# Wider spectrum products on VectorE and joined small steps in a 2-layer FFT-attention and FFN kernel

## The reference, cut to what matters

```python
qf = fft(q, axis=2); kf = fft(k, axis=2)
corr = ifft(qf * conj(kf), axis=2).real
w, idx = top_k(corr.transpose(0, 1, 3, 2), topk)
w = softmax(w, axis=-1)
for i in range(topk):
    g = minimum(idx[:, :, None, :, i] + pos, L - 1)
    out = out + w[:, :, None, :, i] * take_along_axis(v, g, axis=2)
x = x + out
```

## Time and profile before

| what | value |
|---|---|
| median of 3 runs (lowest to highest) | 2646.56 us (2642.76 to 2648.35) |
| span of the profiled execution, first to last instruction | 2644.4 us |
| PE busy | 2497.7 us, 94% |
| POOL busy | 2155.5 us, 82% |
| DVE busy | 1901.7 us, 72% |
| ACT busy | 1055.7 us, 40% |
| DMA traffic | 613.19 MB, 232 GB/s mean |

### The profile page before, as it was taken

The page is one execution under the profiler, slowest core; times in us unless marked ns, Lnnn a source line. Parts: engine busy times, 40 slices in busy tenths (PEclk is TensorE's granted clock), DMA queues, the critical chain, the costliest instruction groups (busy, mean ns, idle before and its releaser), DMA issues.

```text
span 2644.4 us, 36606 instructions
## 1 busy us (share of the span) xinstructions
PE 2497.7 (94%) x12288; PEld 1559.9 (59%) x12288; DVE 1901.7 (72%) x4966; ACT 1055.7 (40%) x1906; POOL 2155.5 (82%) x1558
## 2 busy tenths in 40 slices
PE   4999866799999999999999999999999999999998
PEld 3655555566666656666666666666666666654444
DVE  5989989778787788777877788778876688645000
ACT  4788855533443343533443334533333233201000
POOL 5799999778998799988998899888998899654222
PEclk8999978899999999999999999999999999999999
DMA  9399998966788687966887687957786687758853
GB/s 325 99 261 269 269 244 198 231 192 209 254 266 228 219 252 238 277 203 210 258 270 210 217 275 248 271 181 236 253 250 172 219 265 243 199 203 301 268 180 114
DMA packets 550028, 613.19 MB, mean 232 GB/s; under 512 B 322640, under 2 KB 448720, under 8 KB 532176
## 3 DMA queue, kind: packets, MB, share of 16 engines
q1 hardware_dynamic: 549840, 610.86, 76.6%
HBM read 383.22 MB, written 151.00 MB: 202 GB/s over the span
## 4 chain that ended last, share of the span: by engine, by line
PE 53%; POOL 22%; DVE 8%; DMA 7%; SPq 5%; issue 4%; ACT 1%; POOLq 0%; DVEq 0%; ACTq 0%
PE f_ps L840 11%; PE f_ps L844 11%; PE f_ps L842 11%; PE a_ps L718 7%; PE a_ps L805 5%; PE a_ps L763 4%; POOL a_zu L1115 4%; POOL f_x1p L1115 4%; POOL a_rows L1115 3%; DMA a_w_lag<-a_w_row 2%; PE a_ps L821 2%; PE a_ps L820 2%; POOL a_zv L1115 2%; POOL a_zf L1115 2%; PE a_ps L768 1%
## 5 line engine op out<-in xcount | busy, mean ns | idle before, releaser
L840 PE MATMUL f_ps<-f_whi,f_hhi 128*128 128x512 f16 x2048 | 777.3, 380 | 5.6 <-issue 2.4
L844 PE MATMUL f_ps<-f_whi,f_hlo 128*128 128x512 f16 x2048 | 777.4, 380 | 0.0
L842 PE MATMUL f_ps<-f_wlo,f_hhi 128*128 128x512 f16 x2048 | 777.4, 380 | 0.0
L924 ACT ACTIVATE a_side<-a_ps 128x256 f32<-128x256 f32 (+1 forms) x320 | 128.0, 416 | 873.5 <-PE a_ps L805 698.4
L844 PEld LDWEIGHTS f_ps<-f_whi,f_hlo 128*128 128x128 f16 x2048 | 200.6, 98 | 242.3 <-issue 1.1
L842 PEld LDWEIGHTS f_ps<-f_wlo,f_hhi 128*128 128x128 f16 x2048 | 200.7, 98 | 230.8 <-issue 1.1
L840 PEld LDWEIGHTS f_ps<-f_whi,f_hhi 128*128 128x128 f16 x2048 | 200.7, 98 | 220.6 <-issue 6.7
L1115 POOL TENSOR_TENSOR a_prod<-a_prod,a_tf 128x512 f32<-128x512 f32 x128 | 160.2, 1273 | 138.7 <-DVE a_tf L1242 138.7
L1115 POOL TENSOR_TENSOR a_zv<-a_zv,a_tw 128x512 f32<-128x512 f32 x128 | 183.3, 1450 | 100.5 <-DVE a_tf L1242 100.5
L805 PE MATMUL a_ps<-inv,a_prod 128*128 128x256 f32 x1024 | 239.5, 388 | 25.6 <-POOL a_prod L1115 25.6
L1115 POOL TENSOR_TENSOR f_x1p<-f_x1p,f_y 128x512 f32<-128x512 f32 x128 | 172.7, 1381 | 101.0 <-DVE f_y L1242 101.0
(11 more groups left out here) (137 smaller groups left out, 5236.6 us busy)
## 6 DMA issues: line engine op xcount, KB each, us to landing
f_whi<-whi_scratch SPq DMA_DIRECT2D x128, 512.0 KB, 5.1
f_wlo<-wlo_scratch SPq DMA_DIRECT2D x128, 512.0 KB, 6.5
a_rows<-in_x_dram SPq DMA_DIRECT2D x62, 1024.0 KB, 8.7
vs<-in_ctx_dram SPq DMA_DIRECT2D x64, 512.0 KB, 6.2
xs<-in_x_dram SPq DMA_DIRECT2D x64, 512.0 KB, 8.0
parts_scratch<-a_so SPq DMA_DIRECT2D x64, 512.0 KB, 7.5
x_scratch<-a_rows SPq DMA_DIRECT2D x32, 1024.0 KB, 5.1
f_x1p<-x_scratch SPq DMA_DIRECT2D x32, 1024.0 KB, 6.8
```

The costliest lines, as they stand in the source:

```text
L840: nc.tensor.matmul(f_ps[:, t, :], h_hi[q][:, kq, rows_t], w_hi[u % WR][:, :, kq, :], start=(k == 0), stop=False)
L842: nc.tensor.matmul(f_ps[:, t, :], h_hi[q][:, kq, rows_t], w_lo[u % WR][:, :, kq, :], start=False, stop=False)
L844: mm = nc.tensor.matmul(f_ps[:, t, :], h_lo[q][:, kq, rows_t], w_hi[u % WR][:, :, kq, :], start=False, stop=(k == DB - 1))
L924: return nc.scalar.activation(out, source, ACT.Copy, **how)
```

## The change

The five-slot buffers `vk` and `uk` become one buffer `spectra` with two spectra of six slots: cosine even, cosine odd, sine even with row 0 cleared, sine odd, cosine even with row 0 replaced, cosine odd. Slots 0 to 3 are what one PSUM bank (two parts of 256 columns) is multiplied with, slots 2 to 5 what the other bank is. One instruction reads its bank twice (or four times, for both spectra) by a step of zero. So the 16 products of 512 columns become four of 1024 and two of 2048. `zu`, `zv` and `zf` become parts of one tile `z`, and the terms, `prod` and `tq` parts of one tile `terms`.

On GpSimd the four additions over `zv` and `zf` become two over both, the two one-row additions of the last row become one (now all in `add_lower`), and the closing two additions become one. ScalarE copies a bank with one instruction of 1024 columns in place of one of 512 and one of 256. In `largest` and `choose` the two instructions per step for the negated maximum, the scaled sum and the reciprocal become one each, and the four instructions of 254 columns that fold the lags become two of 508 over both groups. Each of these joined steps waits for both groups, and what waits for the step gets both groups at once.

```diff
-                copy(dst[:, 1:3, :], ps[:, 2, :, :])
-                copy(dst[:, 0, :], ps[:, 2, 0, :]).then_inc(moved, 1)
+                copy(dst.rearrange("p (r j) c -> p r j c", j=2)[:, 0:3:2],
+                     ps[:, 2, :, :].unsqueeze(1).broadcast_to([T, 2, 2, CH])).then_inc(moved, 1)
...
-                    act.wait_ge(max_negated, SUB * n + g + 1)
+                    act.wait_ge(max_negated, n + 1)
...
-                    act.wait_ge(share_known, SUB * n + g + 1)
-                    act.wait_ge(lags_folded, SUB * n + g + 1)
+                    act.wait_ge(share_known, n + 1)
+                    act.wait_ge(lags_folded, n + 1)
                     copy(w_row[:, 0, g, :], corr[:, g, :], scale=share[:, g:g + 1]).then_inc(scaled, 1)
...
             def add_lower(n):
 
                 pool.wait_ge(w0_used, 2 * (n + 1))
-                add(zv[:, 0:2, :], tw[:, 0:2, :], ALU.add)
-                add(zv[:, 2:4, :], tw[:, 2:4, :], ALU.subtract).then_inc(z_paired, 1)
-                add(zf[:, 0:2, :], tf[:, 0:2, :], ALU.add).then_inc(zf_added, 1)
-                add(zf[:, 2:4, :], tf[:, 2:4, :], ALU.subtract)
+                sums, parts_z = by_pair(z[:, 4:12, :]), by_pair(terms[:, :, :], 6)
+                add(sums[:, :, 0], parts_z[:, :, 0], ALU.add).then_inc(zf_added, 1)
+                add(sums[:, :, 1], parts_z[:, :, 1], ALU.subtract).then_inc(z_paired, 1)
+                pool.wait_ge(zu_added, n + 1)
                 pool.wait_ge(zf_added, n + 1)
-                add(zf[0:1, 0, :], last[n % LB][0:1, :], ALU.add)
+                pool.wait_ge(last_raised, n + 1)
+                add(z[0:1, 0:9:8, :], last[n % LB][0:1, :].unsqueeze(1).broadcast_to([1, 2, CH]), ALU.add
+                    ).then_inc(zu_raised, 1)
                 pool.wait_ge(z_paired, n + 1)
                 pool.wait_ge(zu_raised, n + 1)
-                add(zu[:, 0:2, :], zv[:, 0:2, :], ALU.add)
-                add(zu[:, 2:4, :], zv[:, 2:4, :], ALU.add).then_inc(z_added, 1)
+                add(zu, zv, ALU.add).then_inc(z_added, 1)
...
+            def product_twice(out, bank, spectrum):
+                halves = lambda t: t.rearrange("p (r j) c -> p r (j c)", j=2)
+                source = ps[:, bank, :, :].rearrange("p j c -> p (j c)").unsqueeze(1).broadcast_to([T, 2, 2 * CH])
+                return product(halves(out), source, halves(spectrum))
+
+            def product_by_both(out, bank, both):
+                source = ps[:, bank, :, :].rearrange("p j c -> p (j c)").unsqueeze(1).unsqueeze(1)
+                return product(out, source.broadcast_to([T, 2, 2, 2 * CH]),
+                               both.rearrange("p s (r j) c -> p s r (j c)", j=2))
...
-                for g in range(SUB):
-                    dve.wait_ge(top_a_found, SUB * n + g + 1)
-                    nc.vector.tensor_scalar(minus_max[:, g:g + 1], top_a[:, g, 0:1], -1.0, None, ALU.mult
-                                            ).then_inc(max_negated, 1)
+                dve.wait_ge(top_a_found, SUB * (n + 1))
+                nc.vector.tensor_scalar(minus_max[:, :], top_a[:, :, 0], -1.0, None, ALU.mult).then_inc(max_negated, 1)
...
-                for g in range(SUB):
-                    dve.wait_ge(far_copied, SUB * n + g + 1)
-                    by_lag, copied = lags_of(corr[:, g, :]), side[:, g, :].rearrange("p (h l) -> p h l", h=2)
-                    near, far = by_lag[:, :, 0, 1:T], by_lag[:, :, 1, 1:T]
-                    nc.vector.tensor_tensor(far, near, copied[:, :, 1:T], ALU.subtract)
-                    nc.vector.tensor_tensor(near, near, copied[:, :, 1:T], ALU.add).then_inc(lags_folded, 1)
+                dve.wait_ge(far_copied, SUB * (n + 1))
+                by_lag = ps[:, 0:2, :, :].rearrange("p g h (a l) -> p (g h) a l", a=2)
+                copied = side[:, :, :].rearrange("p g (h l) -> p (g h) l", h=2)
+                near, far = by_lag[:, :, 0, 1:T], by_lag[:, :, 1, 1:T]
+                nc.vector.tensor_tensor(far, near, copied[:, :, 1:T], ALU.subtract)
+                nc.vector.tensor_tensor(near, near, copied[:, :, 1:T], ALU.add).then_inc(lags_folded, 1)
```

More of the change, by code:

```diff
@@ L171, in inverse_root_of_tile, with by_pair @@
         op.then_inc(link, 1)
+def by_pair(tile, every=4):
+    return tile.rearrange("p (s a) c -> p s a c", a=every)[:, :, 0:4, :].rearrange("p s (r j) c -> p s r (j c)", j=2)
 class Shared:
@@ L287, in flow @@
         idle = sb("a_idle", [1, 8])
-        tq = sb("a_tq", [T, TB, CH])
         tv = sb("a_tv", [T, TB, CH])
-        vk = [sb(f"a_vk{i}", [T, 5, CH]) for i in range(2)]
-        uk = [sb(f"a_uk{i}", [T, 5, CH]) for i in range(2)]
-        prod = sb("a_prod", [T, 4, CH])
-        zu = sb("a_zu", [T, 4, CH])
-        zv = sb("a_zv", [T, 4, CH])
-        zf = sb("a_zf", [T, 4, CH])
+        spectra = [sb(f"a_spectra{i}", [T, 2, 6, CH]) for i in range(2)]
+        z = sb("a_z", [T, 12, CH])
+        zu, zv, zf = z[:, 0:4, :], z[:, 4:8, :], z[:, 8:12, :]
         tu = sb("a_tu", [T, 4, CH])
-        tw = sb("a_tw", [T, 4, CH])
-        tf = sb("a_tf", [T, 4, CH])
-        term = tf
+        terms = sb("a_terms", [T, 12, CH])
+        prod = terms[:, 4:12, :]
+        tq = terms[:, 0:4, :]
         wts = sb("a_wts", [T, SUB, L])
@@ L1154, in add_products @@
                 pool.wait_ge(q_used, 2 * (n + 1))
-                add(prod[:, 0:2, :], term[:, 0:2, :], ALU.add).then_inc(prod_added, 1)
-                add(prod[:, 2:4, :], term[:, 2:4, :], ALU.subtract).then_inc(prod_added, 1)
+                add(prod[:, 0:2, :], prod[:, 4:6, :], ALU.add).then_inc(prod_added, 1)
+                add(prod[:, 6:8, :], prod[:, 2:4, :], ALU.subtract).then_inc(prod_added, 1)
             def add_upper(n):
@@ L1250, in multiply_queries @@
                 dve.wait_ge(q_mm, 2 * n + 1)
-                product(prod[:, 0:2, :], ps[:, 2, :, :], v[:, 0:3:2, :])
-                product(term[:, 2:4, :], ps[:, 2, :, :], v[:, 3:5, :]).then_inc(q_used, 1)
+                product_twice(prod[:, 0:4, :], 2, v[:, 0:4, :]).then_inc(q_used, 1)
                 dve.wait_ge(q_mm, 2 * n + 2)
-                product(prod[:, 2:4, :], ps[:, 3, :, :], v[:, 1:3, :])
-                product(term[:, 0:2, :], ps[:, 3, :, :], v[:, 3:5, :]).then_inc(q_used, 1)
+                product_twice(prod[:, 4:8, :], 3, v[:, 2:6, :]).then_inc(q_used, 1)
             def multiply_upper(n):
-                u = uk[n % 2]
+                u = spectra[n % 2][:, 1]
                 at_least(dve, out_mm, 2 * n)
```

54 lines of the change are left out of this document (20 added, 34 removed).

## The result

The changed kernel takes 2684.27 us (median of 4 runs, 2683.34 to 2691.46), the kernel before beside it 2644.66. The ratio is 1.0154, with a 95% interval of 1.0138 to 1.0169. It is slower by 1.5%, and the prediction, 2640.6 us in a range up to 2652, was wrong in sign and size.

What follows compares the result with a forecast made beforehand. Side engines VectorE and GpSimd bound the first stage, TensorE the middle, the unchanged product the last. First stage +0.8, middle -6.8, last 0: -6.0 us from 2646.6 gives 2640.6 us, range 2631 to 2652, forecast's own 2636 to 2645.

Steps and rivals of the forecast that it cites:

- the price of the small steps: VectorE's joined small steps: negated maximum 0.13 us later; scaled sum and reciprocal save two short instructions, ahead of a wait.
- The products: VectorE's wide products: ten instructions fewer a window, 0.065 us each, save 0.65 us a window.
- the slower rival: A wide product costs as much as the narrow ones it replaces, 1.20 us a step: +10, 2656.6 us; chance 13%.
- the rival by which the whole fixed part is saved: Each VectorE product start costs its whole fixed part, 0.15 us: -22, 2624.7 us; chance 4%.
- the sign of the slower rival: A first stage longer by 5 us or more would show that wide products cost as much as narrow ones.
- the upper end: Upper bound of the saving on VectorE's products: 0.15 us for each join, 1.5 us a window.
- The fold: VectorE's joined fold waits for both halves, so ScalarE starts scaling later and the weights come 0.82 us later.
- the clock of one window: Middle stage: of two windows with a lowered TensorE clock, 18 and 26, one keeps the full clock: -1.7 us.
- The whole sum: All stages together: first +0.8, middle -6.8, last 0, total -6.0 us on a span of 2644.4.
- the six third windows: Middle stage, third window of each eight: row addition 0.90 us earlier, -5.4 us, and one clock kept, -1.7.
- the first stage: Until 514 us: VectorE's loop +0.17 us in ten windows, +1.7, GpSimd -0.9 in two windows, together +0.8 us.
- GpSimd's additions: Joined additions on GpSimd save 0.46 us a window, with bounds of 0 and 0.7.

Runs made afterwards that it cites:

- e1: The changed kernel with the joined negated maximum and scaled sum each split into two one-column instructions, all else joined: 2645.39 us, 0.9995 of the kernel before.
- e4: The changed kernel with the joined negated maximum and scaled sum as scalar_tensor_tensor instructions that also read a PSUM operand: 2644.14 us, 0.9993 of before.
- e2: The changed kernel with all small steps and the fold by group as before; wide products, copies and GpSimd's joined additions stay: 2643.22 us, 0.9989 of before.
- e10: The kernel of e2 measured again, in five rounds: 2647.76 us, 0.9984 of before.
- e12: The kernel of e2 with one wait more on GpSimd, its lower additions on the upper ones just ahead: 2644.55 us, 0.9989 of before.
- e9: The kernel of e2 with GpSimd's additions unjoined as before, plus a wait of its lower additions on the one-row addition just ahead: 2641.76 us, 0.9961 of before.
- e11: The kernel before with only one wait added, GpSimd's lower additions on the one-row addition just ahead: 2649.27 us, 1.0008 of before.
- e7: The kernel of e3 with four more waits on GpSimd in each window, each on the neighbour just ahead: 2846.81 us, 1.0766 of before.
- e3: The kernel before with only the negated maximum and the scaled sum each joined into one two-column instruction: 2883.82 us, 1.0897 of before.

## Why the prediction was wrong

**The step that failed** is the price of the small steps: the joined negated maximum at "0.13 us later (one step of a tiny instruction; at least 0, at most the 0.28 of two)", and the scaled sum as a saving of a short instruction. They measured 1.07 and 1.50 us, up to 2.3 and 4.35, and e1 shows that this alone is the difference. The bounds were taken as sums of durations at the old operand shape. What had to be asked of each joined instruction was whether it now uses something that the one-column form did not.

**The rows were there.** I cited the PSUM form of L1394, 2279 ns, and passed over its neighbour with both inputs in SBUF, and over what stood beside it in window 34 of the kernel before (group, VectorE, GpSimd):

```profile
L1394 DVE TENSOR_TENSOR f_rowlo<-a_rows,f_rowhi 128x2048 f16<-128x2048 f32 x28 | 78.8, 2813 | 33.5 <-ACT f_rowhi L924 33.5
```

```profile
1289.91 2.28 DVE L1394 TENSOR_TENSOR f_rowlo<-a_rows,f_rowhi 128x2048 f16<-128x2048 f32 x1
```

```profile
1290.07 3.25 POOL L1115 TENSOR_TENSOR a_zv<-a_zv,a_tw 128x512 f32<-128x512 f32 x1 [3.23 <-DVE a_tf L1242]
```

One form has 2813 ns and the other 2279 for the same columns. And GpSimd's addition takes 3.25 us where its like takes 1.26, since it stands still until VectorE's instruction ends. Two engines held each other up before the change too: in that kernel's last stage two low parts take 5.12 and 5.59 us. A rival "the joined step must wait for GpSimd" could have been priced from it: up to 4.5 us where a row addition runs.

**The products** came out as taken. Two of 1024 columns take 2.36 us together and one 1.22, so a step is 2.36 - 1.22 = 1.14 us (I said 1.13), and the step of 2048 columns is 216.67 - 214.47 = 2.20:

```profile
214.47 2.29 DVE L1241 TENSOR_TENSOR a_z<-a_ps,a_spectra 128x2048 f32<-128x2048 f32 x1
216.67 2.28 DVE L1241 TENSOR_TENSOR a_terms<-a_ps,a_spectra 128x2048 f32<-128x2048 f32 x1
...
241.00 2.36 DVE L1241 TENSOR_TENSOR a_terms<-a_ps,a_spectra 128x1024 f32<-128x1024 f32 x2 [0.79 <-PE a_ps L719]
```

That refutes the slower rival (a step of 1.20), whose sign came true by another mechanism, and the rival by which the whole fixed part is saved. I had named a first stage longer by 5 us as the sign of the slower rival; it came, 17.2 us, and pointed at the wrong cause. The section of the Trainium skill that I cited for the upper end, "The DRAIN you can't avoid", also says that a next operation that is not held starts earlier. I had left that out; the starts 0.08 to 0.09 us before the recorded end of the one before agree with it.

**The fold and the rest.** The fold came out as taken: counted from the start of `correlate`, ScalarE starts `a_w_row` at 14.45 us in the kernel before and at 15.29 in e1 (window 22), 0.84 us later where I had 0.82. So did the clock of one window. In e4, window 26 keeps the full clock and is busy for 36.47 us where it was 38.15:

```profile
955.38:995.41 40.03, 36.47 (x185) 23.06 (x184) 30.14 (x63) 14.79 (x25) 34.51 (x21) 1.00 0.92 292
```

What these add up to is not borne out. The whole sum was -6.0 us. Against the span of the kernel before, 2644.4, e4 has 2640.9 and e1 2646.1, and over runs both are within 0.1% of before. One trace each doesn't tell more, because single windows differ by as much. For the six third windows, where I had -7.1 us, the sum is 238.5 us before, 235.1 in e4, and 243.5 in e1, which has a low part of 10.24 us ahead of window 42 (43.2 us long, 38.4 in e4); it is 238.5 and 240.9 in e2 and e10, which are one kernel. For the first stage I had +0.8. Up to window 13 it is 471.8 us before, 474.1 in e1 and 475.5 in e4 with the joined fold, 469.3 and 468.9 in e2 and e10 without it. Window 13 takes 42.4 before and 39.7, 40.1, 42.9 and 40.6 in these four. That e1's first stage as a whole, 513.8 us, lies near the 515.0 that I had is luck.

**GpSimd's additions.** I had 0.46 us a window saved. The lengths are near what I took (2351 ns for 1024 columns, 1256 for the joined one-row addition), but no gain in time is shown for them: e12 with the joins (0.9989) is not faster than e9 without (0.9961).

## What to carry to other kernels

Before joining small instructions, ask of the joined form whether it uses a port, a bank or a queue that the narrow ones did not, and look in the trace for an instruction of the same kind that takes longer beside one engine than alone. In these kernels that was a `tensor_scalar` of two columns with input and output in SBUF, and a `tensor_tensor` with both inputs in SBUF: such an instruction is to be counted with the GpSimd instructions that run then. A width of one kept it free, and so did a `scalar_tensor_tensor` with an operand in PSUM. Where it can't be avoided, a wait in GpSimd's stream at the very place where it starts can pay (e9); elsewhere it gave nothing (e11, e12) or moved the wait to another instruction (e7).

## What the hardware showed that I had not expected

- A `tensor_scalar` of 128x2 f32 from SBUF to SBUF waited for GpSimd (mean 1.07 and 1.50 us, in e3 up to 10.04 us); of 128x1 it took 0.15 us beside the same GpSimd, a `reciprocal` of 128x2 from SBUF to SBUF 0.17 us (all 64), and a `scalar_tensor_tensor` of 128x2 with a PSUM input 0.16 us.
- The wait does not end with GpSimd's running instruction. In e3 it was passed over at 200 ends where the next instruction started 0.03 us or more early, and at none of 67 with a pause of 0.08 us. The section "SBUF: two separate sides" of the Trainium skill's "SBUF — State Buffer" lets one expect a wait for the one instruction that runs; the 9.54 us, past the ends of five, show more, and the measurement decides.
- It goes both ways: a `tensor_tensor` of VectorE with two SBUF inputs adds some 2 us, its own length, to a GpSimd addition that starts beside it (3.25 for 1.26 us).
- Two pairs of joined steps cost 237 us in one kernel and 39 in another with nearly the same work. What such a wait costs depends on the place in GpSimd's stream where it falls, and so on every other instruction's length.
